# First layer's selective scan: whole-piece scans, two decay buffers, column sources read in short rows, two copies of z, all weights at once, merges on every other step, loop written out

## The reference, cut to what matters

```python
x0 = z.reshape(B, D_INNER, L)                                   # by rows
x1 = jnp.swapaxes(z, 2, 3).reshape(B, D_INNER, L)               # by columns
xs = jnp.stack([x0, x1, jnp.flip(x0, -1), jnp.flip(x1, -1)], axis=1)
...
delta = jax.nn.softplus(dts + dt_projs_bias[None, :, :, None])
dA = jnp.exp(delta[..., None] * A[None, :, :, None, :])
dBu = delta[..., None] * Bt[:, :, None] * xs[..., None]
_, hs = jax.lax.associative_scan(combine, (dA, dBu), axis=3)    # h = dA * h + dBu
y = jnp.einsum('bkdln,bkln->bkdl', hs, Ct) + Ds.reshape(K, D_INNER)[None, :, :, None] * xs
...                                                             # each direction turned back
ym = (y0 + y1 + y2 + y3).reshape(B, D_INNER, H, W).astype(x.dtype)
```

## Time and profile before

| quantity | value |
|---|---|
| median of three runs | 1698.62 us |
| the profiled execution's own time | 1702.24 us |
| its span in the profile | 1700.5 us |
| scan phase: first matmul to last sum on POOL | 219.57 to 552.40 us |
| DVE busy over the whole span | 1299.4 us (76%) |
| PE, ACT, POOL busy over the whole span | 1292.2, 1165.6, 966.8 us |

### The profile page before, as it was taken

One profiled execution on the slowest core, in us unless ns is written; L12 is line 12 of the kernel. 1 busy time (PEld: TensorE's weight loads), 2 busy tenths in 40 slices (PEclk: granted clock), 3 DMA queues, 4 the chain that ended last, 5 costly groups with the idle time before them and its releaser, 6 DMA issues. The chain is left out here.

```text
span 1700.5 us, 15968 instructions
## 1 busy us (share of the span) xinstructions
PE 1292.2 (76%) x3822; PEld 437.8 (26%) x3822; DVE 1299.4 (76%) x1358; ACT 1165.6 (69%) x1790; POOL 966.8 (57%) x507
## 2 busy tenths in 40 slices
PE   4999557485574387756788888889889888875996
PEld 2444101011010255532222222222222222111663
DVE  0655459799798277730599999999999999993675
ACT  2676258577584277746888888888988888730564
POOL 2400037869679232202889888888888888850000
PEclk8999855555555699977698888988888888555997
DMA  5344230200200233312877777777777776733562
GB/s 154 93 142 140 75 120 1 89 12 2 99 0 37 68 94 93 96 34 86 198 168 170 175 173 177 177 177 178 179 174 171 172 165 151 159 68 85 125 171 69
DMA packets 137249, 200.40 MB, mean 118 GB/s; under 512 B 27331, under 2 KB 69573, under 8 KB 136394
## 3 DMA queue, kind: packets, MB, share of 16 engines
q1 hardware_dynamic: 135380, 196.94, 46.7%
q10 hardware_dynamic: 1798, 2.68, 0.6%
HBM read 145.93 MB, written 53.63 MB: 117 GB/s over the span
## 5 line engine op out<-in xcount | busy, mean ns | idle before, releaser
L1785 DVE TENSOR_TENSOR_SCAN m_h<-m_qa,m_state,m_ub 128x512 f32<-128x512 f32 x384 | 463.9, 1261 | 15.6 <-POOL m_ub L1397 11.0
L1397 POOL TENSOR_TENSOR m_ub<-m_dlb,m_bt 128x1536 f32<-128x1536 f32 x128 | 438.5, 3446 | 17.1 <-DVE m_h L1785 12.7
L1746 ACT ACTIVATE m_qa<-m_dlb,k_a 128x512 f32<-128x512 f32 x384 | 253.7, 681 | 86.2 <-DVE m_h L1785 85.0
L1142 POOL TENSOR_TENSOR b_u<-b_dl,b_z 128x1024 f32<-128x1024 f32 x48 | 125.8, 2623 | 210.2 <-DMA b_z<-scratch_z 163.3
L1599 PE MATMUL m_qc<-m_bcr,k_selc 32*128 32x512 f32 x256 | 165.9, 731 | 95.6 <-DVE m_g L1796 95.3
L1796 DVE TENSOR_TENSOR m_g<-m_h,m_qc 128x1536 f32<-128x1536 f32 x128 | 221.5, 1730 | 7.8 <-issue 3.5
L1616 PE MATMUL m_qy<-m_g,k_seld 128*32 128x512 f32 x768 | 176.3, 772 | 0.0
L979 PE MATMUL b_qb<-b_bc,k_pack_sel 96*128 96x512 bf16 x96 | 78.6, 819 | 108.1 <-DVE b_u L1063 108.1
L1037 ACT ACTIVATE b_qa<-b_dl,b_a 128x512 f32<-128x512 f32 x96 | 65.5, 684 | 91.4 <-DVE b_h L1078 78.5
L1542 PE MATMUL m_qf<-m_cva,k_conv 113*96 113x504 f32 (+1 forms) x192 | 104.9, 689 | 18.5 <-DMA m_cvb<-scratch_xpad 18.5
L1078 DVE TENSOR_TENSOR_SCAN b_h<-b_qa,b_h,b_u 128x512 f32<-128x512 f32 x84 | 106.9, 1272 | 0.1
(11 more groups left out here) (184 smaller groups left out, 2623.0 us busy)
## 6 DMA issues: line engine op xcount, KB each, us to landing
m_dlb<-scratch_dldu SPq DMA_DIRECT2D x128, 384.0 KB, 10.3
m_bt<-scratch_brow SPq DMA_DIRECT2D x128, 256.0 KB, 5.9
scratch_dldu<-m_dldu SPq DMA_DIRECT2D x32, 384.0 KB, 3.2
scratch_z<-a_z SPq DMA_DIRECT2D x24, 256.0 KB, 5.9
b_z<-scratch_z SPq DMA_DIRECT2D x3, 2048.0 KB, 8.6
scratch_y<-b_yrow SPq DMA_DIRECT2D x12, 512.0 KB, 2.8
c_y<-scratch_y SPq DMA_DIRECT2D x16, 384.0 KB, 3.4
scratch_gate<-m_gt SPq DMA_DIRECT2D x32, 192.0 KB, 3.6
```

Of the source, the lines that this page charges most:

```text
L1142: nc.gpsimd.tensor_tensor(by_column(u[s][:], col), by_column(dl[s][:], col), seen(z[:], col, piece), ALU.mult).then_inc(u_ready, 1)
L1397: nc.gpsimd.tensor_tensor(ub[k % 3][:], dlb[u % 2][:, J:2 * J, :], bcast(bt[u % 2][:, n, :], J), ALU.mult).then_inc(ub_ready, 1)
L1746: nc.scalar.activation(q_a[:, j, :], dlb[u % 2][:, j, :], ACT.Exp, scale=G["a1"][:, j, n:n + 1]).then_inc(da, 1)
L1785: nc.vector.tensor_tensor_scan(h[k % 3][:, j, :], q_a[:, j, :], ub[k % 3][:, j, :], state[:, k % NS, j:j + 1], ALU.mult, ALU.add).then_inc ...
```

## The change

- **Scan**: one scan of 1024 instead of two of 512; `b_qa` becomes two whole tiles, and to make room in PSUM `b_qdt` becomes one tile instead of two. `dt_of` of a step now waits until delta of the step just before is finished. The decay is one ACT instruction of 1024.
- **Order**: on DVE, `delta_of` moves from the head of a step to between the halves. On ACT the decay of the step before comes ahead of the softplus, also from third to third. On PE, `dt_of` comes after the four spreads.
- **Column sources**: matmuls of a column direction now read runs of 8 neighbouring elements, 64 runs, and write each run into PSUM with a stride of 64 elements.
- **z twice**, by turns, and loaded a third ahead; **weights, A and D of all thirds** loaded at the start, where ACT and DVE wait for A and D before anything else.
- **First loads**: the broadcasting loads of `b_dt` become six plain ones; SP no longer waits for them before it issues z and the B and C rows.
- **Merges**: at sums 0, 2, 4 and 6 of the eight row sums of a third, where they stood at sums 0 to 3.
- **Loop**: the thirds are written out.

```diff
-        q_dt = [m.ps(f"b_qdt{s}", [P, TC]) for s in range(2)]
+        q_dt = m.ps("b_qdt", [P, TC])
         q_b, q_c = m.ps("b_qb", [P, CH]), m.ps("b_qc", [P, CH])
-        q_a = m.ps("b_qa", [P, 2, CH])
+        q_a = [m.ps(f"b_qa{s}", [P, TC]) for s in range(2)]
...
+        def seen_rows(tile, col, piece, v):
+
+            if not col:
+                return seen(tile, col, piece, TC // CH, v)
+            start = (piece * TC + v * CH) // H
+            return tile.rearrange("p (h w) -> p h w", h=H)[:, :, start:start + CH // H]
+
+        def by_rows(ap, col):
+
+            return ap.rearrange("p (w h) -> p h w", h=H) if col else ap
...
-                row = 0
-                for part in range(3):
-                    count = X_PARTS.count(part)
-                    src = D["dt0"][part, DTR * k:DTR * k + DTR, :].unsqueeze(0).broadcast_to([count, DTR, T])
-                    sp.dma_start(dtx[k][row:row + count * DTR, :], src).then_inc(dt_loaded[k], 16)
+                for g, part in enumerate(X_PARTS):
+                    sp.dma_start(dtx[k][DTR * g:DTR * g + DTR, :], D["dt0"][part, DTR * k:DTR * k + DTR, :]).then_inc(dt_loaded[k], 16)
...
             load_dt(order[0][0])
-            sp.wait_ge(w_loaded, nw)
-            sp.wait_ge(dt_loaded[order[0][0]], 64)
             load_z(0)
             sp.dma_start(bcx[:], D["bc0"].rearrange("a r t -> (a r) t")).then_inc(bc_loaded, 16)
             for k, _, _ in order[1:]:
                 load_dt(k)
+            load_z(1)
...
-                pe.wait_ge(delta, freed(i))
+                pe.wait_ge(delta, freed(i, 1))
                 for v in range(TC // CH):
-                    last = nc.tensor.matmul(by_column(q_dt[s][:, v * CH:v * CH + CH], col), wdt[:, k, :],
-                                            seen(dtx[k][:], col, piece, TC // CH, v), start=True, stop=True)
+                    last = nc.tensor.matmul(by_rows(q_dt[:, v * CH:v * CH + CH], col), wdt[:, j, k, :],
+                                            seen_rows(dtx[k][:], col, piece, v), start=True, stop=True)
...
-            act.dma_start(a0[:], D["l0_alog"][0]).then_inc(a_loaded, 16)
-            act.dma_start(ds[:], D["l0_Ds"][0]).then_inc(a_loaded, 16)
-            with act.Fori(0, J) as j:
+            act.dma_start(a0[:], D["l0_alog"].rearrange("j p k -> p j k")).then_inc(a_loaded, 16)
+            act.dma_start(ds[:], D["l0_Ds"].rearrange("j p k -> p j k")).then_inc(a_loaded, 16)
+            act.wait_ge(a_loaded, 32)
+            nc.scalar.activation(a0[:], a0[:], ACT.Exp).then_inc(a_exp, 1)
+            act.wait_ge(a_ready, 1)
+            for j in range(J):
                 for st in range(n + 1):
+                    if st > 0:
+                        i, s = j * n + st - 1, (st - 1) % 2
+                        act.wait_ge(delta, done(i))
+                        k = steps[st - 1][0]
+
+                        act.wait_ge(scanned, freed(i))
+                        nc.scalar.activation(q_a[s][:], dl[s][:], ACT.Exp, scale=a0[:, j, k:k + 1]).then_inc(da_ready, 1)
                     if st < n:
...
-                    if st + 1 < n or more:
-                        delta_of(i + 1, 1 - s)
                     for o, v in in_order(steps[st][2]):
                         drive(i, s, o, v)
                         if st > 0:
                             times_c(j, st - 1, o)
-                        scan(i, s, o, v, steps[st][2], steps[st][4])
+                        if o == 0 and (st + 1 < n or more):
+                            delta_of(i + 1, 1 - s)
+                    scan(i, s, steps[st][2], steps[st][4])
...
-                        if not col and st - 2 < 3 * NTC:
-                            merge(j, piece)
-                            pool.wait_ge(merged, NTC * j + piece + 1 + LEAD)
+                        if not col:
+                            m, odd = divmod(st - 2 - 2 * NTC, 2)
+                            if odd == 0:
+                                merge(j, m, steps[3 * NTC + m][3])
+                            pool.wait_ge(merged, NTC * j + m + 1 + LEAD)
```

More of the change, by code:

```diff
@@ L870, in scan0_phase @@
         n = len(steps)
+        z_loaded = [m.sem(f"b_z_loaded{r}") for r in range(2)]
         dt_loaded = [m.sem(f"b_dt_loaded{k}") for k in range(K4)]
@@ L978, in spread @@
                 pe.wait_ge(used, half(j * n + st, o) - 1)
[L979 to L980 removed]
+                nc.tensor.matmul(by_rows(q[:], col), G["selbc0"][:, row + k, :],
+                                 seen_rows(bcx[:], col, piece, v), start=True, stop=True).then_inc(ready, 1)
             def turn(j, more):
                 for st in range(n + 1):
[L985 to L988 removed]
                     for o in range(2):
@@ L993, in turn @@
                             spread(j, st - 1, o, q_c, K4, read, c_mm)
+                    if st + 2 < n:
+                        dt_of(j, st + 2)
+                    elif more and st < n:
+                        dt_of(j + 1, st + 2 - n)
             dt_of(0, 0)
@@ L997, in _ @@
             pe.wait_ge(bc_loaded, 16)
-            with pe.Fori(0, J - 1) as j:
+            for j in range(J - 1):
                 turn(j, True)
@@ L1133, in merge @@
                                         ALU.add).then_inc(merged, 1)
-            with pool.Fori(0, J) as j:
-                pool.wait_ge(z_loaded, 16 * j + 16)
+            for j in range(J):
+                pool.wait_ge(z_loaded[j % 2], 16 * (j // 2) + 16)
                 for st in range(n + 2):
```

122 lines of the change are left out of this document (43 added, 79 removed).

## The result

The changed kernel took 1723.68 us, the median of four runs (1718.80 to 1731.21); the kernel before took 1698.88 us beside it, also the median of four. The ratio is 1.0152, with a 95% interval of 1.0106 to 1.0198: 1.5% slower. The forecast was 1687.0 and the range ended at 1705; both the size and the sign were wrong.

A forecast was written before the change was run, and what follows sets the result against it. The prediction took DVE as the bound in plain steps and POOL in merging row steps. From 1702.24 us it took 11.2 (thirds) and 0.4 (start), giving 1690.6; from the median, 1698.62 - 11.6 = 1687.0, range 1675 to 1705.

The forecast's parts named there:

- The start: Kernel start: A and D land at 226, first drive at 234.3 us, 0.4 earlier; bounds 223.5 and 238.
- 17 more 8 KB loads with their marks, 5.6 us: At the start: the other 34 packets of A and D pass beside these loads in 5.6 us.
- from about 212: At the start: estimated time packets of A and D flow, after seven issues of 0.4 us and 1.5 us more.
- near 221: At the start: landing time of the B and C rows, which before the change landed at 231.96 us.
- rival 3: At the start: A and D not held back, fast columns, first drive at 224, total 1677 us; chance 0.15.
- So the column matmuls decide: Column steps: m, PE time of one 512 matmul, decides whether the loop exceeds 5.75 us; taken as 0.43 to 0.5.
- rival 1: Column matmuls: strided write costs what the strided read did, m = 0.86, +3 us net, total 1702; chance 0.25.
- Plain steps: Scan-phase steps without a merge: one 1024 scan of 2.25 us replaces two, step becomes 5.75 us, 0.12 less.
- ring of 4.8 + 2m: Loop over the one `b_qdt` through matmuls, softplus and delta: 5.66 us at m = 0.43, 6.5 at m = 0.86.
- Merges: Row steps with a merge on POOL: three distances of 6.85 us instead of 7.6, 0.8 less each.
- From third to third: Turn between thirds: 14.2 us to the next drive, 21.1 with the step before it, for 22.3 before the change.
- Rival 2: Column matmuls: strided write costs more and PE is the bound, 1780 us at m = 1.7, about 1718 at 1.2; chance 0.12.

## Why the prediction was wrong

- **The start** is the step that cost most. The prediction had A and D land at 226 and the first drive at 234.3, 238 at worst; it was 257.16. Its mechanism held (one for one, 50 packets an engine). The term "17 more 8 KB loads with their marks, 5.6 us" was mis-sized: it took 0.33 us for each from the earlier trace rows, which were two engines' packets in a load of another form. The plain rows took 0.90 us each with twelve or so of them under way, and the last 34 turns 17.9 us: 12.3 of the 21.9 us by which A and D were late, counted from SP's first issue. Another 7.4 lie in "from about 212": the first packet of A went after 11.7 us and not after 4.4. What holds a first packet back so long stays open. The first 16 turns added 2.0. The bound was wrong for the same reason: I varied what stands ahead, and never the time of a turn.
- **B and C** would have been late too: "near 221" is 13.4 us after SP's first issue, and with A and D out of the way they landed after some 22. So rival 3's first drive at 224, 16.4 us after that issue, was out of reach; it came after 23.1.
- **"So the column matmuls decide"** is the second. "I take 0.43 to 0.5" should have been 0.86, by the prediction's own working from a pair: rival 1 came true, with a chance of 0.25. Its 15 us were 14.5, the difference that the plain writes make. That its sum, "+3", is also what the phase lost from the first drive on (3.0 us) is partly luck: 1.7 us of these are the first distance, longer by the late start, and without the strided write the phase saves 317.7 - 304.6 = 13.1 us and not 11.2. The argument from the half clock was no argument: a stride in the write doubles the matmul at that clock, as one in the read does.
- The Trainium skill had both sides of it. "PSUM — Partial Sum Buffer", Specifications (TRN2), has any non-contiguous access slow a matmul significantly, and the trace agrees: 1.89 us with the strided write, 1.03 with the plain one. "SBUF — State Buffer", the note under The DMA port swizzle, lets runs of 8 bf16 elements be read at full rate, and the trace agrees, with 1.03 us. "DMA: Bandwidth & Descriptors", Queues, rings and completion order, has a packet hold some 9 to 17 descriptors, by which A and D would pass in three to six turns (an estimate, for 48 pieces an engine; the prediction said two or three). Here every piece of 16 bytes was a packet and had a turn of its own.
- **Plain steps** were right: 5.75 forecast, 5.76 measured; scan 2.25 and 2.26. So was the ring of 4.8 + 2m: 6.5 at m = 0.86, measured 6.6.
- **Merges**: 6.85 forecast, 6.67 measured. **From third to third**: 14.2 forecast, 14.33 measured, by the right number for a reason that is only half right: the last product of DVE, the sum and u are as long a chain as merge, sums and u.
- Put together: with plain writes a third takes 102.8 us, where the prediction had 103.8. Its account of the thirds was good but for m, and its account of the start but for the time of a turn and the time of the first packets.
- Rival 2 did not come: PE is not the bound even with strided writes, since moving the pair in PE's order brings the steps back to 5.76. Rival 3 did not come either. No case had the start as slow as it was, which is why the range missed: rival 1 alone would have ended inside it.
- The whole miss is 24.8 + 11.6 = 36.4 us. The start makes 21.6 of it (first drive 48.2 us after SP's first issue, forecast 26.7), the strided write 14.5 and the first distance 1.7; the rest of the phase was 1.9 us better than forecast. That is 35.9.

## What to carry to other kernels

Count what a first wait stands behind in packets, queue by queue, and price a turn by the load that will be on the other queue, not by one of another form; a small transfer that everything waits for goes ahead of the large ones. When a stride can't be avoided, put it where an engine reads at its own pace for free, here DVE's and ACT's reads of PSUM, not on PE's read or write. And where a buffer is given up, draw the ring that closes through the remaining one and ask how each link would do at twice its length.

## What the runs showed of the hardware

- 768 pieces of 16 bytes have landed 3.2 us after the second issue with nothing ahead, and 36.8 us after it behind the weights and beside loads of 8 KB rows: each piece is a packet and takes turns one for one.
- A packet of 8 KB took 0.90 us in loads of 12 rows side by side, 0.75 to 0.85 us with nothing beside them (closing marks included), 0.48 with the rows ten partitions apart and issued half as fast, 0.53 in one transfer of 72 rows, and 0.34 in the broadcasting form, which kept about three engines busy (72 GB/s).
- At a granted clock of 0.50 a pair of 512-column matmuls takes 1.03 us with a plain write and runs of 8 bf16 elements read, 1.89 with a float32 write of stride 64; before the change it took 1.90 with a plain write and a read of stride 64.
- A float32 read of PSUM with a stride of 8 or 16 elements costs DVE and ACT nothing (delta 1214 ns, drive 674, absolute value 1023).
